# The attention's output in a fused attention and feed-forward kernel: one 64-column PSUM sum, scaled by VectorE

## The reference

```python
x = x + _L0_xattn_ref(_layernorm(x, axis=-1), ctx_2048, ctx_2048)
x = x + _L0_ffn_ref(_layernorm(x, axis=-1), pweight, nweight, exps, ...)
# attention, per head, by chunks of keys:
scores = jnp.einsum('bhqd,bhkd->bhqk', q, kj) * SCALE      # causal: -inf above the diagonal
exp_c = jnp.exp(scores - new_m)
out = out * (s / new_s) * exp_old + jnp.einsum('bhqk,bhkd->bhqd', exp_c / new_s, vj)
# linear layer:
soft = jax.nn.sigmoid(temp * pweight) - jax.nn.sigmoid(temp * nweight)
weight = jnp.einsum('oin,n->oi', soft, exps * mask) * scale[0]
return jnp.einsum('bsi,oi->bso', input, weight) + bias
```

## Time and profile before

| what | value |
|---|---|
| median of 3 runs | 1215.75 us (1213.83 to 1216.52) |
| the profiled execution | 1213.7 us, its span 1211.9 us |
| TensorE's mean granted clock | 0.982 |
| instructions | 28076 |
| HBM read, written | 67.15 MB, 16.78 MB |

### The profile page before, as it was taken

The page is one execution under the profiler, slowest core; times in us unless marked ns, Lnnn a source line. Parts: engine busy times, 40 slices in busy tenths (PEclk is TensorE's granted clock), DMA queues, the critical chain, the costliest instruction groups (busy, mean ns, idle before and its releaser), DMA issues. The chain is left out here.

```text
span 1211.9 us, 28076 instructions
## 1 busy us (share of the span) xinstructions
PE 1109.8 (92%) x10788; PEld 803.6 (66%) x10788; DVE 968.1 (80%) x1424; ACT 922.2 (76%) x1898; POOL 687.4 (57%) x766
## 2 busy tenths in 40 slices
PE   4787889899999999889999999999999999899988
PEld 3676756566666776666766777676776676677753
DVE  5756677888888887888888887888888788888862
ACT  6899866688787787677787787788788787787750
POOL 3465546554446886454446986555348986463251
PEclk8889898999999999999999999999999999999999
DMA  9999726575759786675759886764658986654442
GB/s 317 287 321 330 256 71 118 129 148 108 150 121 175 178 186 130 140 141 106 151 120 201 150 191 128 159 158 107 127 119 199 183 173 143 135 105 97 86 88 70
DMA packets 382581, 190.88 MB, mean 158 GB/s; under 512 B 358128, under 2 KB 358128, under 8 KB 378352
## 3 DMA queue, kind: packets, MB, share of 16 engines
q1 hardware_dynamic: 381440, 189.05, 68.1%
q10 hardware_dynamic: 1008, 0.04, 0.1%
HBM read 67.15 MB, written 16.78 MB: 69 GB/s over the span
## 5 line engine op out<-in xcount | busy, mean ns | idle before, releaser
L533 ACT ACTIVATE p<-slot,mx 128x512 f32<-128x512 f32 (+7 forms) x512 | 378.0, 748 | 142.8 <-DVE mx L647 89.9
L647 DVE TENSOR_REDUCE mx<-slot 128x1 f32<-128x640 f32 (+7 forms) x352 | 356.8, 1016 | 32.4 <-PE slot L417 30.5
L464 PE MATMUL ffnb<-wt,yt 128*128 128x512 f16 x1464 | 373.0, 381 | 3.1 <-DVE ring L709 1.7
L653 DVE SCALAR_TENSOR_TENSOR pt<-ptb,pt 128x512 f16<-128x512 f32 (+1 forms) x504 | 281.9, 599 | 102.7 <-ACT pt L549 102.3
L413 PE MATMUL slot<-kt,qt 128*128 128x128 f16 (+3 forms) x1056 | 268.6, 284 | 16.4 <-ACT p L533 10.9
L414 PE MATMUL slot<-kt,qs 128*128 128x128 f16 (+3 forms) x1056 | 268.2, 284 | 0.0
L549 ACT ACTIVATE pt<-ptb 128x512 f16<-128x512 f32 (+1 forms) x504 | 239.9, 528 | 30.4 <-PE ptb L427 28.1
L427 PE MATMUL ptb<-id,p 128*128 128x128 f32 x1700 | 241.1, 280 | 12.2 <-DVE pt L653 10.4
L870 POOL TENSOR_TENSOR att<-osb 128x256 f32<-128x256 f32 x128 | 97.9, 765 | 271.0 <-ACT osb L556 266.4
L464 PEld LDWEIGHTS ffnb<-wt,yt 128*128 128x128 f16 x1464 | 136.9, 98 | 103.1 <-DVE ring L709 2.8
L446 PE MATMUL oacc<-v,pt 128*128 128x128 f16 x1700 | 180.3, 221 | 24.9 <-ACT osb L556 10.6
(11 more groups left out here) (90 smaller groups left out, 1451.1 us busy)
## 6 DMA issues: line engine op xcount, KB each, us to landing
ring<-in_x_dram SPq DMA_DIRECT2D x32, 512.0 KB, 4.3
cin<-in_ctx_dram SPq DMA_DIRECT2D x32, 512.0 KB, 4.6
out_dram<-ring SPq DMA_DIRECT2D x32, 512.0 KB, 3.4
qs<-qt SPq DMA_DIRECT2D x124, 128.0 KB, 2.9
v<-in_weights_dram SPq DMA_DIRECT2D x11, 1024.0 KB, 7.2
kt<-in_weights_dram SPq DMA_DIRECT2D x11, 1024.0 KB, 7.9
pd<-in_weights_dram SPq DMA_DIRECT2D x5, 1024.0 KB, 6.9
yt<-in_weights_dram SPq DMA_DIRECT2D x5, 1024.0 KB, 8.6
```

The costliest lines, as they stand in the source:

```text
L464: last = pe.matmul(dst, yt[:, k % 2, a * KT_N + kk, :], wt[:, c, kk, half * 512:half * 512 + 512], start=r == 0, stop=r == 3 * KT_N - 1)
L533: last = nc.scalar.activation(p32[:, j.par, hh * j.keys:(hh + 1) * j.keys], slot[:, j.par, base:base + j.keys], ACT.Exp, bias=mx[:, j.par, ...
L647: nc.vector.tensor_reduce(mx[:, j.par, 0:j.heads], src[:, 0:j.heads, 0:j.keys], AX_X, ALU.max, negate=True).then_inc(mx_ready, 1)
L653: nc.vector.scalar_tensor_tensor(pt[:, j.par, j.blocks + blocks.start:j.blocks + blocks.stop, :], ptb[:, c % 2, 0:P * len(blocks)].rearran ...
```

## The change

For each block of keys `values` makes three matmuls of 64 columns instead of one of 128 and one of 64: high with high, high with low, low with high, all onto the same 64 columns of the group's accumulator, which now takes half of the bank (`obank` is the bank, `oacc` its first 256 columns). ScalarE's copy is gone, and `osb` with it. VectorE's `reciprocals` becomes `output`: the reciprocals, a wait for them, for the values of the group and for GpSimd's addition two groups back, and one operation that multiplies the 256 sums by 1/1024 and by the reciprocals, from PSUM to `att` in SBUF, of which there are now two. That operation sets `osb_done`. GpSimd only adds `att` to the residual rows.

```diff
--- before.py
+++ after.py
@@ -195,8 +195,7 @@
         qs = sb("qs", [P, H, P], F16)
         p32 = sb("p32", [P, 2, 8 * P], F32)
         pt = sb("pt", [P, 2, 2 * 8, P], F16)
-        osb = sb("osb", [P, 2, GROUP, 2 * D], F32)
-        att = sb("att", [P, GROUP, D], F32)
+        att = sb("att", [P, 2, GROUP, D], F32)
         y16 = sb("y16", [P, 2, KT_N, P], F16)
         yt = sb("yt", [P, 2, 2 * KT_N, P], F16)
         bias_row = sb("bias_row", [P, DM], F32)
@@ -244,8 +243,11 @@
 
         slot = stack.enter_context(nc.psum_tensor("slot", [P, 2, 1024], F32))
         ptb = stack.enter_context(nc.psum_tensor("ptb", [P, 2, 512], F32))
-        oacc = stack.enter_context(nc.psum_tensor("oacc", [P, GROUP, 2 * D], F32))
+        obank = stack.enter_context(nc.psum_tensor("obank", [P, 4, P], F32))
         ffnb = stack.enter_context(nc.psum_tensor("ffnb", [P, 512], F32))
+
+
+        oacc = obank[:, 0:2, :].rearrange("p a b -> p (a b)").rearrange("p (h d) -> p h d", d=D)
 
         first_kt = slot[:, 0, :].bitcast(F16).rearrange("p (h c) -> p h c", c=P)
         first_qt = slot[:, 1, :].bitcast(F16).rearrange("p (h c) -> p h c", c=P)
@@ -264,8 +266,8 @@
         s_done, mx_ready, p_done = sem("s_done"), sem("mx_ready"), sem("p_done")
         t_done, hi_done, lo_done, pv_done = sem("t_done"), sem("hi_done"), sem("lo_done"), sem("pv_done")
         p16_hi, p16_lo, pt_in = sem("p16_hi"), sem("p16_lo"), sem("pt_in")
-        osb_done, osb_added = sem("osb_done"), sem("osb_added")
-        rinv_ready, att_ready, x1_ready = sem("rinv_ready"), sem("att_ready"), sem("x1_ready")
+        osb_done = sem("osb_done")
+        rinv_ready, x1_ready = sem("rinv_ready"), sem("x1_ready")
         q_stats, q_mv, q_rs, q_norm, q_hi, q_lo = (sem("q_" + n) for n in ("stats", "mv", "rs", "norm", "hi", "lo"))
         y_stats, y_mv, y_rs, y_norm, y_hi, y_lo = (sem("y_" + n) for n in ("stats", "mv", "rs", "norm", "hi", "lo"))
         c_hi, c_lo = sem("c_hi"), sem("c_lo")
@@ -443,10 +445,12 @@
                     for blk in range(j.i + 1):
                         k = hh * (j.i + 1) + blk
                         v = v16[:, (j.t - j.i + blk) % V_PLACES, h]
-                        pe.matmul(oacc[:, h % GROUP, :], turned[:, k, :], v,
-                                  start=blk == 0, stop=False, skip_group_check=True)
-                        last = pe.matmul(oacc[:, h % GROUP, 0:D], turned[:, j.blocks + k, :], v[:, 0:D],
-                                         start=False, stop=blk == j.i, skip_group_check=True)
+                        dst = oacc[:, h % GROUP, :]
+                        pe.matmul(dst, turned[:, k, :], v[:, 0:D], start=blk == 0, stop=False, skip_group_check=True)
+                        pe.matmul(dst, turned[:, k, :], v[:, D:2 * D], start=False, stop=False,
+                                  skip_group_check=True)
+                        last = pe.matmul(dst, turned[:, j.blocks + k, :], v[:, 0:D], start=False, stop=blk == j.i,
+                                         skip_group_check=True)
                 last.then_inc(pv_done, 1)
 
             def linear(k, m0, m1, spare=None):
@@ -470,7 +474,7 @@
                 pe.wait_ge(bias_step, 18)
                 pe.wait_ge(osb_done, JOBS[BIAS_JOBS[r] - 2].group + 1)
                 for k in range(4):
-                    last = pe.matmul(oacc[:, k, :], ones32[:, :], bdiag[:, 4 * r + k, :], start=True, stop=True)
+                    last = pe.matmul(obank[:, k, :], ones32[:, :], bdiag[:, 4 * r + k, :], start=True, stop=True)
                 last.then_inc(bias_summed, 1)
 
             def weights(u):
@@ -550,12 +554,6 @@
                                          ptb[:, c % 2, 0:P * len(blocks)].rearrange("p (k c) -> p k c", c=P),
                                          ACT.Copy, scale=P_SCALE).then_inc(hi_done, 1)
 
-            def output(g):
-                act.wait_ge(pv_done, LAST_OF_GROUP[g] + 1)
-                reached(act, osb_added, g - 1)
-                nc.scalar.activation(osb[:, g % 2], oacc[:, :, :], ACT.Copy, scale=1.0 / P_SCALE
-                                     ).then_inc(osb_done, 1)
-
             def q_split(t):
                 act.wait_ge(q_norm, t + 1)
                 if t == 1:
@@ -582,7 +580,7 @@
             def bias_part(r):
                 act.wait_ge(bias_summed, r + 1)
                 nc.scalar.copy(bias_row[:, :].rearrange("p (q j) -> p j q", j=8)[:, 4 * r:4 * r + 4, :],
-                               oacc[:, :, :]).then_inc(bias_out, 1)
+                               obank[:, :, :]).then_inc(bias_out, 1)
 
             def weights_high(u):
                 act.wait_ge(w_summed, 2 * u + 2)
@@ -619,8 +617,6 @@
                     weights_high(j.n - 1)
                 if j.n - 1 in BIAS_JOBS:
                     bias_part(j.n - 1 - BIAS_JOBS[0])
-                if j.n > 1 and JOBS[j.n - 2].closes_group:
-                    output(JOBS[j.n - 2].group)
                 high_parts(j)
                 if j.n + 1 < UNITS:
                     chunk_tanh(2 * j.n + 2)
@@ -634,7 +630,6 @@
                     c_split(t + 2)
                 if q_at(t, s, 2):
                     q_split(t + 2)
-            output(GROUPS * TILES - 1)
             for k in range(TILES - 1, TILES):
                 y_split(k)
 
@@ -661,12 +656,17 @@
                 nc.vector.scalar_tensor_tensor(p16[:, size:2 * size], p32[:, j.par, 0:size], P_SCALE,
                                                p16[:, 0:size], ALU.mult, ALU.subtract).then_inc(p16_lo, 1)
 
-            def reciprocals(g):
+            def output(g):
                 dve.wait_ge(p_done, LAST_OF_GROUP[g] + 1)
-                reached(dve, att_ready, g - 1)
                 h0 = GROUP * (g % GROUPS)
                 nc.vector.reciprocal(rinv[:, g % 2, :], rowsum[:, g // GROUPS % 2, h0:h0 + GROUP]
                                      ).then_inc(rinv_ready, 1)
+                dve.wait_ge(rinv_ready, g + 1)
+                dve.wait_ge(pv_done, LAST_OF_GROUP[g] + 1)
+                reached(dve, x1_ready, g - 1)
+                nc.vector.scalar_tensor_tensor(att[:, g % 2], oacc, 1.0 / P_SCALE,
+                                               rinv[:, g % 2, :].unsqueeze(2).to_broadcast([P, GROUP, D]),
+                                               ALU.mult, ALU.mult).then_inc(osb_done, 1)
 
             def moments(k, t, src, s_stats, s_mv, s_rs):
                 reached(dve, s_rs, 3 * t)
@@ -778,7 +778,7 @@
                 if j.n + 1 < len(JOBS) and JOBS[j.n + 1].d is not None:
                     low_part_unturned(JOBS[j.n + 1])
                 if j.n > 1 and JOBS[j.n - 2].closes_group:
-                    reciprocals(JOBS[j.n - 2].group)
+                    output(JOBS[j.n - 2].group)
                 low_parts(j)
                 if j.n + 1 < UNITS:
                     first_difference(j.n + 1)
@@ -801,7 +801,7 @@
                             result(k, half)
                 for k in y_begun(t, s):
                     y_moments(k)
-            reciprocals(GROUPS * TILES - 1)
+            output(GROUPS * TILES - 1)
             spare = slot[:, 0, 0:512]
             for k in range(TAIL, TILES):
                 if TILES - 2 < k + 2 < TILES:
@@ -865,18 +865,9 @@
 
             def add_attention(g):
                 pool.wait_ge(osb_done, g + 1)
-                reached(pool, x1_ready, g)
-                o = osb[:, g % 2]
-                nc.gpsimd.tensor_tensor(att[:, :, :], o[:, :, 0:D], o[:, :, D:2 * D], ALU.add).then_inc(osb_added, 1)
-                pool.wait_ge(osb_added, g + 1)
-                pool.wait_ge(rinv_ready, g + 1)
-                nc.gpsimd.tensor_tensor(att[:, :, :], att[:, :, :],
-                                        rinv[:, g % 2, :].unsqueeze(2).to_broadcast([P, GROUP, D]),
-                                        ALU.mult).then_inc(att_ready, 1)
-                pool.wait_ge(att_ready, g + 1)
                 c0 = GROUP * D * (g % GROUPS)
                 dst = ring[:, g // GROUPS % RING, c0:c0 + GROUP * D]
-                nc.gpsimd.tensor_tensor(dst, dst, att[:, :, :].rearrange("p h d -> p (h d)"), ALU.add
+                nc.gpsimd.tensor_tensor(dst, dst, att[:, g % 2].rearrange("p h d -> p (h d)"), ALU.add
                                         ).then_inc(x1_ready, 1)
 
             def difference(w):
```

## The result

The changed kernel takes 1186.65 us (median of 4 runs, 1182.88 to 1189.46), the kernel before in the same session 1214.79 us (1212.33 to 1216.52): a ratio of 0.977, with a 95% interval of 0.975 to 0.979. The profiled execution took 1185.72 us, its span 1183.9 us at a mean granted clock of 0.990 (before: 1211.9 us at 0.982). It is read against the earlier trace rows.

The account below looks back on a forecast made before the run. The prediction took TensorE's stream, plus the moments at which it stands still, to bound the kernel over most of the span. Its terms summed to -6.2 us from the median of 1215.75, giving 1209.5 us, range 1194 to 1228.

Parts of the forecast that it names:

- TensorE's pace: Values' matmuls: three short ones at 28 ns each replace a pair of 85 ns, over 2304 pairs: -2.3 us.
- weight stage: Where the weights are made, ScalarE loses copies, five of them made without having waited: -1.5 us, between 0 and -2.5.
- wait after a tile's last group: TensorE's wait for the accumulator there goes, as VectorE's output ends before ScalarE's copy did: -9 us.
- after the first group: In tiles of sixteen steps VectorE has L661 ahead of the output; TensorE's wait grows 0.3 us in 16 tiles: +4.8 us.
- after the second group: VectorE's maxima and reciprocal delay the output: a new TensorE wait of 0.7 us in 24 tiles, +16.8 us.
- L845 moves onto L661: GpSimd's L845, coming sooner, draws out VectorE's low part L661; 0.3 us each for some 12 tiles: +4 us.
- relief by GpSimd and ScalarE: GpSimd's L856 clears L661 and ScalarE's parts come earlier, so TensorE waits less: -19 us, between -5 and -35.
- the bracket in the prediction: Remark on the wait after the second group: 0 if VectorE's queue is ahead by then.
- Rival 2: Short matmuls on TensorE don't keep 28 ns; three take 91.5 ns: 1227 us, 1310 at the upper bound; chance 0.10.
- rival 4: The chain through both engines shortens more, with more relief and new waits half as large: 1187 us; chance 0.10.
- Rival 1: VectorE becomes late, having no reserve at 85%, and relief elsewhere doesn't come: 1227.5 us; chance 0.22.
- the signs named ahead: What the trace should show: matmul starts, new operation's time, values' waits for output, L661's time, ScalarE's and GpSimd's shares.

Follow-up runs that it names:

- experiment 8: Changed kernel with the old pair of 128 and 64 columns for the values, low-half products left out of the result: 1182.86 us, ratio 0.976.
- experiment 12: Kernel of experiment 11 with GpSimd's long splits held back until VectorE has made the next unturned low part: 1177.91 us, ratio 0.972.
- experiment 11: Changed kernel with VectorE's output put ahead of the maxima in steps whose job TensorE does not turn: 1175.60 us, ratio 0.9705.
- experiment 1: Kernel before with GpSimd's three operations per group cut to the one that adds, other engines' work kept: 1197.89 us, ratio 0.988.
- experiment 5: Changed kernel with a 128x512 scratch copy on ScalarE at the old copy's place, waiting for the values' products: 1202.74 us, ratio 0.992.
- 6: Changed kernel with the 128x512 scratch copy on ScalarE at the old place, but without the wait for the values' products: 1206.07 us, ratio 0.994.
- 7: Changed kernel with ScalarE's wait for the values' products at the old place, but a scratch copy of only 4 columns: 1190.29 us, ratio 0.982.
- experiment 3: Changed kernel with two more 128x256 scratch operations on GpSimd ahead of each group's addition: 1228.85 us, ratio 1.014.

## Why the prediction was wrong

The sign and the mechanisms that it named were right, the sum was not. Step by step, in the words of the prediction; what was found is TensorE's idle time, worked out as in the table of the first section, here for all tiles from the fifth on:

| term | predicted, us | found, us |
|---|---|---|
| TensorE's pace | -2.3 | +4.6 (87 instead of 85 ns per block); 3.8 by experiment 8 |
| weight stage | -1.5 | not told apart |
| wait after a tile's last group | -9 | -7.5 |
| after the first group | +4.8 | +1.4 |
| after the second group, 24 tiles | +16.8 | +7.0, all of it in the tiles of sixteen steps |
| L845 moves onto L661 | +4 | about 0, by experiment 12 |
| relief by GpSimd and ScalarE | -19 | -28.6 |

The found terms make -23; some 5 us of the 28 are left. In the traces 3.0 us of the difference lie in the first four tiles, where the weights are made. But its last split ends at 153.8 us before and 152.3 after, and between 148.9 and 156.4 us among the runs here, so this can't be put down to the change. Half clock (granted clock 0.5) is the other part, a term that the prediction didn't have: the stretch from 192.3 us costs up to 3.9 us before the change, 2.6 of them without a wait and so in no row of the table, and in the first 140 us half clock is granted for 34 us before and 20 us after.

**The step that failed most is the new waits.** "24 x 0.7 = +16.8 us" for the second group was +7.0, and with the first group's 3.4 us less than forecast this is 13 us of the miss. The 0.65 us was built on times of the kernel before the change, with VectorE's maxima ending at 842.62. But the reliefs are on the same queue: VectorE runs ahead of those times, the wait of that tile is 0.39 us instead (at 817.72), and the tiles of eight steps have none, as the bracket in the prediction allowed. A wait worked out from a late queue has to be worked out again once another term of the sum has moved that queue. That it is a real wait of VectorE's order is shown by experiment 11, which takes it away.

**The second is the relief**, -19 forecast and -28.6 found. Of the values' wait for low parts 9.7 us went (-10 forecast), of the transposes' wait 3.3 (2.6 forecast). The scores' idle time for exponentials went altogether, 10.8 us where "a quarter" of the earlier trace rows was 6.8; and 4.8 us went that the prediction had not priced, waits for parts turned by DMA and for VectorE in the linear layer, both of which come behind other work on VectorE's queue. The prediction had ScalarE come in only as "ScalarE's parts come 0.5 us earlier". The runs show two reliefs of like size: GpSimd's is 15 us on the kernel before (experiment 1), ScalarE's time is 16 us on the changed kernel (experiment 5, and 6 against 7), because it stood ahead of the high parts in a chain in which VectorE and TensorE wait in turn. The row for it was there: VectorE's low parts waited 1.57 us for ScalarE's high parts at 819.29.

**L845**, +4: its overlap with an unturned low part did come (L656 took 1.77 us in that tile at 822.06), but experiment 12 takes it away, on the kernel of experiment 11, and wins nothing that can be told, so TensorE seems not to have waited for it.

**The pace went the other way**, 7 us worse than forecast. The 28 ns behind a short matmul in the earlier trace rows held for three in a row but for 1 ns (in the means, at full clock and without waits, 87.6 ns per block against 85.1). Rival 2's mechanism is real at less than half of its assumed size (87 against 91.5 ns per block), and far from its bound. The Trainium skill ("TensorE: Matmul & The Clock Gate", Back-to-back issue gap) gives about 81 ns for a matmul of 128 columns in a stream with weight loads. These runs disagree: it is 57 ns in the kernel before, and three weight loads and three matmuls of 64 columns take 87 ns together after the change.

So **rival 4** came nearest, forecast at 1187 us with a chance of 0.10: all of the low parts' wait, half of the others, and the new waits half as large. Its mechanism is the one found, but that it meets the time to 1 us is luck in part: it had 33 us of relief where 28.6 were found, and a pace 7 us too fast, and its sum takes 8 us off the new waits, which were 13 us less than forecast.

**Rival 1 was not wrong but conditional.** It said that the change is slower if the relief does not come, "where the relief is under 13 us", at 1227.5 us. Experiment 3 is that case for GpSimd's part of the relief: 1228.9 us. ScalarE's part stays in it, so the agreement in the number does not confirm the rival's terms. The four kernels side by side, medians in us:

| | GpSimd with three operations | with one |
|---|---|---|
| outputs by ScalarE's copy | 1214.8 (before) | 1197.9 (experiment 1) |
| outputs by VectorE from PSUM | 1228.9 (experiment 3) | 1186.7 (after) |

Moving the output alone loses 14 us, with GpSimd relieved it wins 11. (Experiment 1 has the pair of 128 and 64 columns, a difference of about 4 us.) The two parts of the change can't be priced one by one and added. The Trainium skill ("VectorE: DVE Perf Modes", Two Vector instructions with no wait between them) says that an instruction with two tensor inputs in SBUF reads the second through an interface shared with GpSimd. The traces agree: with GpSimd's old load L656 is drawn out to 2.48 us, and so are VectorE's other long operations with both inputs in SBUF (L700, 128x1024, took 1.21 us alone and up to 2.36 us in the changed kernel), while the output with its input in PSUM took 0.424 us in the mean of all.

Of the signs named ahead, GpSimd's share came at 42% and ScalarE's at 73% (70 forecast), the new operation at 0.42 us, the low part in the fourth step at 1.09 us. The values waited 0.62 us after the first group and 0.39 us after the second in that tile, where 0.9 and 0.7 were given (the prediction's own working, 0.44 of before and 0.3 more, makes 0.74 for the first).

## What to carry to other kernels

Where several engines hand a tile to one another in turn, half a microsecond taken from one in front of its part of the chain can be worth more than its idle time suggests: ask what stands right behind the removed instruction, and follow its result to the engine that sets the pace. When an operation moves onto another engine's queue, look first at what stands ahead of it there; here two operations in another order were worth 11 us, 40% as much as the whole change. And where two effects touch the same queue, price them together, or build the corner cases and time them.
